# A transformer block on one Trainium2 core: one of eight splits of the attention outputs goes from GpSimd to VectorE, and two scattered sends move across a block's border

## The reference

```
x = x + self_attention(layernorm(x))           # 16 heads of 64
x = x + cross_attention(layernorm(x), context) # 16 heads of 16, 361 keys
x = x + experts(x)                             # each token: 1 of 8 experts
```

## Time and profile before

| | us |
|---|---|
| median of 3 runs (lowest, highest) | 1476.35 (1476.33, 1479.77) |
| the profiled execution | 1477.7 |
| its span, first to last instruction | 1475.8 |
| mean granted clock of TensorE | 0.977 of full speed |

### The profile page before, as it was taken

The page is one execution under the profiler, slowest core; times in us unless marked ns, Lnnn a source line. Parts: engine busy times, 40 slices in busy tenths (PEclk is TensorE's granted clock), DMA queues, the critical chain, the costliest instruction groups (busy, mean ns, idle before and its releaser), DMA issues. The chain is left out here.

```text
span 1475.8 us, 39048 instructions
## 1 busy us (share of the span) xinstructions
PE 1372.4 (93%) x12162; PEld 1192.2 (81%) x12162; DVE 950.5 (64%) x2409; ACT 761.4 (52%) x1882; POOL 651.4 (44%) x1001
## 2 busy tenths in 40 slices
PE   6999999999999999859999999999999976999997
PEld 5888888887878787847888888888888865888887
DVE  5757575757575666436777777777777754655554
ACT  5747474746565565514665656565565631222222
POOL 5534344352626171732345555555555541333332
PEclk9999999999999999978999999999999987999999
DMA  6607162524334252537767777677766652666662
GB/s 195 156 1 169 30 145 51 127 69 107 89 85 111 66 130 59 141 103 206 190 176 193 192 194 187 176 193 192 196 187 175 178 189 82 227 214 215 209 220 70
DMA packets 181116, 217.44 MB, mean 147 GB/s; under 512 B 83486, under 2 KB 148933, under 8 KB 180774
## 3 DMA queue, kind: packets, MB, share of 16 engines
q1 hardware_dynamic: 176424, 209.60, 52.2%
q0 software_dynamic: 3584, 6.58, 1.4%
q10 hardware_dynamic: 1024, 0.21, 0.1%
HBM read 137.62 MB, written 79.43 MB: 147 GB/s over the span
## 5 line engine op out<-in xcount | busy, mean ns | idle before, releaser
L1478 DVE TENSOR_REDUCE row_max<-psb_s 100x1 f32<-100x361 f32 x512 | 265.5, 530 | 143.5 <-PE psb_s L1694 137.8
L1348 ACT ACTIVATE probs<-psb_t 121x400 f32<-121x400 f32 (+1 forms) x384 | 190.5, 508 | 88.3 <-PE psb_t L1704 82.2
L541 POOL TENSOR_TENSOR diag<-neg_ident,row_max 100x400 fp32r<-100x400 f32 x128 | 112.9, 903 | 260.0 <-DVE row_max L634 231.3
L1694 PE MATMUL psb_s<-k,q 97*100 97x362 f32 x512 | 185.2, 364 | 15.3 <-DVE row_max L1478 7.7
L1704 PE MATMUL psb_t<-q,k 98*121 98x200 f32 (+1 forms) x768 | 146.4, 273 | 1.7 <-ACT probs L1348 1.7
L1704 PEld LDWEIGHTS psb_t<-q,k 98*121 98x121 f32 (+1 forms) x768 | 125.7, 184 | 4.5 <-ACT probs L1348 2.4
L454 ACT ACTIVATE probs<-ps_t 100x400 f32<-100x400 f32 x128 | 57.5, 501 | 113.2 <-PE ps_t L791 113.2
L1694 PEld LDWEIGHTS psb_s<-k,q 97*100 97x100 f32 x512 | 85.8, 168 | 35.5 <-DVE row_max L1478 18.0
L2181 ACT ACTIVATE hid<-psd_h,b_sb 128x256 f32<-128x256 f32 (+1 forms) x100 | 43.2, 432 | 113.7 <-PE psd_h L2295 113.6
L1717 PE MATMUL psb_o<-probs,v_ext 121*32 121x100 f32 (+1 forms) x3072 | 92.8, 253 | 0.0
L309 ACT COPY q_t<-ps_p 64x200 f32<-64x200 f32 x112 | 57.4, 512 | 63.6 <-PE ps_p L66 62.8
(11 more groups left out here) (255 smaller groups left out, 3738.1 us busy)
## 6 DMA issues: line engine op xcount, KB each, us to landing
w_sb<-in_w SPq DMA_DIRECT2D x28, 1024.0 KB, 7.5
routed_rows<-empty SPq DMA_DIRECT2D x7, 3855.0 KB, 19.8
packed_keys<-k_st SPq DMA_DIRECT2D x32, 724.0 KB, 4.4
k<-packed_keys SPq DMA_DIRECT2D x64, 362.0 KB
v_rows<-v_tok SPq DMA_DIRECT2D x32, 400.0 KB
v_ext<-v_rows SPq DMA_DIRECT2D x32, 400.0 KB
q<-packed_queries SPq DMA_DIRECT2D x64, 200.0 KB
w_third<-in_w SPq DMA_DIRECT2D x12, 1024.0 KB, 7.7
```

The source lines that it names most:

```text
L541: pool.tensor_tensor(diag[:, g % 2], c.neg_ident[0:S, 0:S].unsqueeze(1).to_broadcast([S, GH, S]), row_max[:, g // 2 % 2, g % 2].unsqueeze( ...
L1348: act.activation(probs[0:KT[kt], u % 2, kt], ps_t[i % 2][0:KT[kt], 0:4 * S], ACT.Exp, scale=HD2 ** -0.5).then_inc(probs_ready, 1)
L1478: dve.reduce_max(row_max[:, p, h:h + 1], ps_s[h % 2][0:S, 0:S2], AX_X).then_inc(max_ready, 1)
L1694: pe.matmul(ps_s[h % 2][0:S, 0:S2E], q2[0:97, p, u, g, S * a:S * (a + 1)], k2[0:97, p, u, g], start=True, stop=True).then_inc(scores_ready, 1)
```

## The change

It does two things.

First, the split of round 3's outputs (`DVE_SPLITS = GB - 1 = 3`) is made by VectorE in a new function `split_last`, in iteration 6, behind `next_input` and ahead of the wait for the projection. GpSimd makes the other seven of a group; its counts go through `split_by_pool`. TensorE's first projection and ScalarE's copies of round 5 wait for the new semaphore `last_split`.

Second, the sends of the last two sequences (30 and 31) leave the cross-attention's block: GpSimd issues them in the experts' block, between `roots(0)` and `residual(0)`. The waits for all sends leave that block too; SP has them at the head of its list in the experts' block, ahead of the loads of tile 2.

```diff
@@ self_attention
+        DVE_SPLITS = GB - 1
+
+        def split_by_pool(q, r):
+
+            return q * (ROUNDS - 1) + (r + 1 - (r >= DVE_SPLITS))
@@ scalar, iteration r
+                        elif r - 4 == DVE_SPLITS:
+                            act.wait_ge(last_split, q * 2 + 2)
                         else:
-                            act.wait_ge(o_lo_ready, q * ROUNDS + (r - 3))
+                            act.wait_ge(o_lo_ready, split_by_pool(q, r - 4))
@@ gpsimd
-                    if r >= 3:
+                    if r >= 3 and r - 3 != DVE_SPLITS:
                         split_outputs(q, r - 3)
@@ vector
+            def split_last(q, r):
+
+                s0 = SQ * (r % GB)
+                hi, lo = (t[:, :, :, s0:s0 + SQ] for t in (o_hi, o_lo))
+                src = o_part[:, r % 2].rearrange("p g (s t) -> p g t s", t=NT)
+                dve.wait_ge(ot_copied_act, q * 2 * GQ + 4 * (r + 1))
+                dve.sem_inc(dve_passed, 1)
+                dve.tensor_copy(hi, src).then_inc(last_split, 1)
+                dve.wait_ge(last_split, q * 2 + 1)
+                dve.tensor_tensor(lo, src, hi.bitcast(F32), ALU.subtract).then_inc(last_split, 1)
...
                     if r == INPUT_AT and not last:
                         next_input(q + 1)
+                    if r - 3 == DVE_SPLITS:
+                        split_last(q, r - 3)
@@ tensor
-                            pe.wait_ge(o_lo_ready, q * ROUNDS + (r - 2))
+                            pe.wait_ge(o_lo_ready, split_by_pool(q, r - 3))
+                            if r - 3 == DVE_SPLITS:
+                                pe.wait_ge(last_split, q * 2 + 2)
@@ cross_attention, sync
-            for p in range(2):
-                sp.wait_ge(routed[p], 16 * (B // 2))
@@ cross_attention, gpsimd
             for n in range(B - 3, B):
                 add_counts(n, n % 2)
-                send_last_rows(n - 1)
-            send_last_rows(B - 1)
-            for p in range(2):
-                pool.wait_ge(routed[p], 16 * (B // 2))
+                if n < B - 1:
+                    send_last_rows(n - 1)
@@ experts, sync
+            for p in range(2):
+                sp.wait_ge(c.routed[p], 16 * (B // 2))
             for j in range(TILES - 2):
@@ experts, gpsimd
             roots(0)
+            for n in (B - 2, B - 1):
+                send_rows_of(pool, c, n, xs)
             residual(0)
```

More of the change, by code:

```diff
@@ L53 @@
 EARLY_BATCHES = B - 6
+LAST = 5
 EARLY = -(-(S * EARLY_BATCHES - E * (T - 1)) // T)
@@ L247, in self_attention @@
         o_lo_ready = sem("o_lo_ready")
+        last_split = sem("last_split")
         y_ready = sem("y_ready")
@@ L529, in split_outputs @@
                 pool.tensor_copy(hi, src).then_inc(o_hi_ready, 1)
-                pool.wait_ge(o_hi_ready, q * ROUNDS + (r + 1))
+                pool.wait_ge(o_hi_ready, split_by_pool(q, r))
                 pool.tensor_tensor(lo, src, hi.bitcast(F32), ALU.subtract).then_inc(o_lo_ready, 1)
@@ L857, in cross_attention @@
         KP = KT[0]
-        LAST = 5
         wq_sb, wk_st, wv_st, wo_sb = c.wq_sb, c.wk_st, c.wv_st, c.wo_sb
@@ L910, in cross_attention @@
         last_f = sb("last_f", [S, 1])
-        last_slots = sb("last_slots", [S, LAST], U32)
+        last_slots = c.last_slots
         ps_p = [psum(f"psb_p{i}", [128, 512]) for i in range(2)]
@@ L981, in cross_attention @@
         slot_ready = sem("slot_ready")
-        routed = [sem(f"routed{p}") for p in range(2)]
+        routed = c.routed
         last_placing = sem("last_placing")
@@ L1229, in send_last_rows @@
                     pool.wait_ge(routed[n % 2], 16 * (EARLY_BATCHES // 2))
-                pool.indirect_dma_start(
-                    out=xs, out_offset=bass.IndirectOffsetOnAxis(ap=last_slots[:, n - (B - LAST):n - (B - LAST) + 1],
-                                                                 axis=0),
-                    in_=c.x[:, n, :], in_offset=None).then_inc(routed[n % 2], 16)
+                send_rows_of(pool, c, n, xs)
             def routing(b, p):
@@ L1885, in table_buffers @@
 def table_buffers(nc, c, ctx):
+    c.last_slots = ctx.enter_context(nc.sbuf_tensor("last_slots", [S, LAST], U32))
+    c.routed = [ctx.enter_context(nc.semaphore(f"routed{p}")) for p in range(2)]
     c.totals = ctx.enter_context(nc.sbuf_tensor("totals", [1, 2, E], F32))
@@ L2032, in load_rows, with send_rows_of @@
     sp.dma_start(c.rows[:, j % 3, 0:nh], src).then_inc(c.rows_loaded[j % 3], 16)
+def send_rows_of(pool, c, n, xs):
+    at = n - (B - LAST)
+    pool.indirect_dma_start(out=xs, out_offset=bass.IndirectOffsetOnAxis(ap=c.last_slots[:, at:at + 1], axis=0),
+                            in_=c.x[:, n, :], in_offset=None).then_inc(c.routed[n % 2], 16)
 def load_weights(sp, c, j, w1_dst, w2_dst, w1, w2):
```

## The result

The changed kernel takes **1513.19 us** (median of 4 runs, 1512.14 to 1513.29); the kernel before took 1476.34 in the same comparison (4 runs, 1475.7 to 1479.77). The ratio is **1.0234**, 95% interval 1.0213 to 1.0254: slower, as forecast, by 36.9 us where 28.4 were forecast, and 1.2 us above the range.

A forecast was written before the change was run, and what follows sets the result against it. TensorE, busy 93% of the span, was taken to bound the kernel. Waits +26.6, clock +9.2, last group -1.2 and earlier experts -6.2 gave +28.4 us: 1504.8 us, 1.9% slower, range 1494 to 1512.

The forecast's parts named there:

- The direction and the mechanism: Groups 0 to 6: VectorE's split stands behind its wait for `rstd`, so TensorE's first projection starts 3.8 us later; kernel slower.
- The split's own time: VectorE's cast 0.45 and subtraction 0.52 us with gaps 0.1, 1.07 in all, within +3.8 us a group, +26.6 in seven.
- Rival (e): VectorE's split takes 2.27 us on a path shared with GpSimd, each group 1.2 us later: 1513.2 us; chance 0.05.
- The clock: First projections of groups 0 to 6 begin at half clock after the wait; one already paid, six new: 6 x 1.54 = +9.2 us.
- Rival (a): TensorE's clock does not fall more often than now at the first projections: 1495.6 us; chance 0.12.
- Group 7: Last group, no next input: VectorE splits straight after round 4's scaling, TensorE's wait of 1.3 us goes nearly whole: -1.2 us.
- The border: Between cross-attention and experts: the barrier no longer waits for the last sends to land, experts start earlier: -6.2 us.
- what a barrier costs by itself shows between the first two blocks: VectorE's idle time of 0.32 us at the first barrier, taken as the price of the one before the experts.
- Rival (b): Start of the experts: no gain, as another wait (SP's loads, tile 2's late rows) replaces the landing: 1511.0 us; chance 0.10.
- (c): First projections: VectorE's split is ready when TensorE comes to it, so TensorE never waits: 1459.8 us; chance 0.05.
- (d): GpSimd's 2.25 us saved in iteration 6 moves the next group forward and covers the delay: 1470 to 1477 us; chance 0.04.

The follow-up runs named there:

- The delay alone: Kernel before the change, with TensorE's first projection in groups 0 to 6 also waiting for the next group's `xn`: 1520.77 us, ratio 1.0285.
- the split alone: Changed kernel with the last two sequences' sends and their waits back in the cross-attention's block, round 3's split still on VectorE: 1516.85 us, ratio 1.0275.
- TensorE kept warm: Changed kernel with 40 unused matmuls on TensorE ahead of its wait for the split in groups 0 to 6: 1501.52 us, ratio 1.0171.
- the sends alone: Changed kernel with round 3's split back on GpSimd, the sends and their waits staying in the experts' block: 1472.63 us, ratio 0.9975.
- VectorE late: The sends alone, plus six unused `bn_stats` behind VectorE's last cast to slots in the cross-attention's block: 1474.3 us, one execution.
- the load moved: The sends alone, with tile 1's weight loads moved to the head of SP's list in the experts' block: 1473.09 us, ratio 0.9974.
- the split ahead: Changed kernel with `split_last` placed ahead of `next_input` in VectorE's list, nothing else: 1465.1 us, ratio 0.9922.
- run 17: Not a label but part of "run 17 times": the unchanged kernel before, executed 17 times in one comparison, 1472.92 to 1480.17 us.

## Why the prediction was right, and where it was off

**The direction and the mechanism** held. The split moved in front of TensorE's projection and behind VectorE's wait for `rstd`; `xn` was forecast at 226.34 on group 2's scale and came at 237.91 - 11.57 = 226.34 (11.57 being by how much the shift of round 5, and GpSimd's `diag` behind it, are later now). The delay alone costs 43.4 us, the split alone 40.5; the place alone, one edit of order, turns 2.3% slower into 0.8% faster.

**The split's own time was too small a term.** The step was "I take 0.45 and 0.52, with 0.1 for the gaps: 1.07 in all". From `xn`'s end it took 1.4:

```profile
L635 DVE CAST o_hi<-stage x8: 511/515/615, 74.6 to 644.1; 128x400 fp32r<-128x400 f32 x8
L637 DVE TENSOR_TENSOR o_lo<-stage,o_hi x8: 872/875/884, 75.1 to 644.8; 128x400 fp32r<-128x400 f32 x8
```

(least, median and longest, in ns.) The cast was right within 0.07. The subtraction was scaled by length from one with 1024 elements, and took 0.875 instead of 0.52. That one has the same types; this one reads `stage` through a rearranged view and writes 25 of every 100 places of `o_lo`. Whether that is why was not measured. It makes each wait 4.05 us longer instead of 3.8: 28.4, not 26.6. Rival (e), which gave the pair 2.27 us for a shared path, was wrong at this place, where GpSimd is idle and the pair takes 1.4. Its figure of 1513.2 is the measured time by accident. Of what it rested on, the 1.28 us for GpSimd's subtraction is 1.23 in the earlier trace rows, and the slow cast in the earlier trace rows has one SBUF input, so it says nothing of two.

**The clock** was forecast at six times 1.54, 9.2; measured 9.7, with the size per group 1.46 to 1.93. Rival (a) is out, and the run with TensorE kept warm shows that this is clock and not, say, late operands. To take group 5's slow projection as the price was right. To count on exactly one group as already paid was luck: the wait of 1.3 us is the same in four profiled kernels, and half clock followed in group 5 of the kernel before, in no group of the sends alone, in group 2 with VectorE late (7.28 us) and in group 0 with the load moved (7.29).

**Group 7** gained 0.8, not 1.2: the same longer subtraction.

**The border** gave 5.0 instead of 6.2 in the profiled execution, and 3.7 by the medians. The step "what a barrier costs by itself shows between the first two blocks", 0.32 us, failed: this border costs 1.6 to 3.8 us with the sends gone, and in the four kernels with 2.8 to 3.8 us behind VectorE's last cast the loads of tile 1's weights are still under way then. Rival (b), that it gives nothing, is wrong, but its reason, SP's loads in the place of the landing, holds for a part. The change shows only 1.6 us there because its last sequences took 3 us longer, so that the loads were through 0.4 us before VectorE finished; the 5.0 of the border and the 3.4 below hang together. An estimate: at full clock in that step its border would be near the 2.8 to 3.8 of the other kernels, and the fall there cost some 1 to 2 us net. Why 1.6 us stay even with the load moved away is open: the releaser named is TensorE's sequencer, though TensorE's last matmul ends 1.0 us before VectorE's last cast in the changed kernel.

**What was not foreseen** is the 3.4 us in cross-attention, the largest single error: a step of the last sequences (3.0 us) ran for the most part at half clock in the changed kernel and not before. With the 1.8 of the waits, 0.5 of the clock, 0.4 of group 7, 1.2 of the border and 0.2 less elsewhere in sum, it makes up the 7.1 us between the forecast 28.4 and the span's 35.5. The sum had no term for it: it let every stretch but the first projections and the border stand as it was. The same stretch of the last sequences in the profiled executions of all ten kernels: 12.26 to 12.27 us in seven, 13.61 with the split alone, 13.75 with the load moved, 15.24 in the change. So it is no cost of the split as such: with TensorE kept warm, the delay alone or the split ahead, the step takes 12.27. Nor need it belong to the kernel: the kernel before, run 17 times in one comparison, takes 1478.0 us and more in the six executions with a mean clock of 0.975 or less, up to 1480.17, and 1477.0 and less in the other eleven, down to 1472.92. So the clock differs from execution to execution of one kernel, by several us. The change's four executions lie within 1.2 us; whether all of them have the slow step is open, since only one of them shows it. The range should have had some 3 us for that at its upper end.

**The other rivals.** (c), faster, named its own condition, "ahead of the statistics or without the wait for `rstd`", and forecast 1459.8 for that; the kernel which meets it takes 1465.1, since 4.2 of the 10.4 us of waits stay and the border gives 3.8 instead of 6.2. (d), that GpSimd's saved time pays back, is wrong: `rstd` moved forward by 1.7 us, which takes 1.7 off a wait that would else be 7.0, and GpSimd then sat idle for 10.52.

## What to carry to other kernels

When work is moved to another engine, its place in that engine's list matters more than its duration: read which wait stands in front of it, and on whom that wait depends. Here the same two instructions, 1.4 us of work, cost 4.05 us of waiting and 1.4 of clock a group behind one wait, and took 0.8 us off TensorE's wait in front of it. Where the engine that waits is TensorE, count the granted clock as a second term beside the wait, and expect the time to differ by a few us from one execution to the next where there are many short idle times.

## What the runs showed of the hardware

**The clock falls after short idle times too.** Waits of 5.3 us were followed by half clock in all of 7 groups; waits of 1.3 us by half clock in one of 8 before (7.30 us instead of 5.75), in one of 8 with VectorE late, in one of 8 with the load moved and in none of 8 with the sends alone; idle times of 0.46 and 0.79 us in the last sequences by half clock in some executions (1.23 us for 24 matmuls) and full clock in others (0.72), with the same instructions around them. The Trainium skill, "TensorE: Matmul & The Clock Gate", in its part "Why this matters for your kernels", speaks of long gaps alone. The 5.3 us waits agree; the falls behind 1.3 us and less are not among what it describes.

**VectorE's subtraction and GpSimd's `diag` slow each other.** With the split ahead of the next input, they run side by side. GpSimd in group 2 of that kernel, and VectorE's subtraction in group 1:

```profile
219.32 1.67 POOL L552 TENSOR_TENSOR diag<-neg_ident,row_max 100x400 fp32r<-100x400 f32 x2
221.49 2.29 POOL L552 TENSOR_TENSOR diag<-neg_ident,row_max 100x400 fp32r<-100x400 f32 x2 [0.51 <-PE ps_t L815]
```

```profile
145.43 1.36 DVE L637 TENSOR_TENSOR o_lo<-stage,o_hi 128x400 fp32r<-128x400 f32 x1
```

The pair of `diag` that overlaps the subtraction takes 2.29 us, the pair before it 1.67, and it is 2.17 to 2.33 in all seven groups; in the changed kernel, where no subtraction of VectorE's runs beside it, the same pair takes 1.66. In group 1 the subtraction itself takes 1.36 instead of 0.89, beside a pair of 2.17. The Trainium skill, "GPSIMD Engine Reference", Specifications, says that the two share SBUF interfaces and collide when VectorE's instruction has two SBUF inputs, which this one has; the rows agree.

**A border between blocks has no fixed price.** 0.3 us at the first, and at the second 0.62 to 3.77 us behind VectorE's last instruction in kernels whose sends had left it; delaying VectorE by 2.7 us shortened the idle time by 3.2. Where a weight load was still under way when VectorE's last cast was done, in four kernels, the next block began 2.1 to 2.5 us behind the end of the DMA traffic.
